# Attention products as sixteen 32x32 float32 tiles, first scores one batch ahead, row sums on ScalarE

## The reference

```python
row_zero = exp_v.sum(-1) == 0
q_exp = jnp.where(row_zero[..., None], 0.0, q[:, None, :])
self_feat = jnp.concatenate([exp_v, q_exp], -1) @ W_self.T + b_self
for d in range(2):                                   # adjacency and its transpose
    A = (adj_f if d == 0 else swapaxes(adj_f, 1, 2))[:, :, :20, :]
    cond, vb = A.sum(-1), A @ w_bias + b_bias
    kv = self_feat[:, :20]
    qh, kh = heads(self_feat @ Wq.T + bq), heads(kv @ Wk.T + bk)     # 16 heads of 32
    aff = einsum('bnhd,bmhd->bnhm', qh, kh) / sqrt(32)
    w = softmax(where(cond > 0, aff, NEG) + vb)      # over the 20 keys
    output += heads_out(einsum('bnhm,bmf->bnhf', w, kv), Wout) + bout
result = v + relu(self_feat + output)
```

## Time and profile before

| | us |
|---|---|
| time, median of 3 runs | 617.11 (617.08 to 618.52) |
| span of the profiled execution | 616.5 |
| own time of the profiled execution | not recorded; the median lies 0.6 above this span |
| PE busy | 606.8 (98%) |
| DVE busy | 527.0 (85%) |
| POOL busy | 436.2 (71%) |
| ACT busy | 386.7 (63%) |

### The profile page before, as it was taken

The page is one execution under the profiler, slowest core; times in us unless marked ns, Lnnn a source line. Parts: engine busy times, 40 slices in busy tenths (PEclk is TensorE's granted clock), DMA queues, the critical chain, the costliest instruction groups (busy, mean ns, idle before and its releaser), DMA issues.

```text
span 616.5 us, 10667 instructions
## 1 busy us (share of the span) xinstructions
PE 606.8 (98%) x4047; PEld 532.3 (86%) x4047; DVE 527.0 (85%) x770; ACT 386.7 (63%) x737; POOL 436.2 (71%) x400
## 2 busy tenths in 40 slices
PE   9999999999999999999999999999999999999995
PEld 6977898989898988989898898989898989889892
DVE  4898899999797989989797988888897979787675
ACT  4658647877566776757586755668574758653432
POOL 0301388876978886797986688989569798858852
PEclk9999999999999999999999999999999999999999
DMA  8976545846758672657775385857357676726061
GB/s 312 424 284 183 146 109 172 212 183 128 269 113 270 120 263 52 160 194 175 225 165 192 71 237 154 241 143 207 119 121 262 129 251 127 256 53 169 1 147 69
DMA packets 54466, 109.54 MB, mean 178 GB/s; under 512 B 27855, under 2 KB 37583, under 8 KB 47695
## 3 DMA queue, kind: packets, MB, share of 16 engines
q1 hardware_dynamic: 52254, 93.13, 47.7%
q0 software_dynamic: 2160, 15.73, 14.0%
HBM read 88.05 MB, written 20.78 MB: 177 GB/s over the span
## 4 chain that ended last, share of the span: by engine, by line
PE 94%; DVE 3%; POOL 1%; issue 1%; ACT 0%
PE aff L572 36%; PE gen L500 10%; PE gen L502 9%; PE gen L501 9%; PE aff L540 8%; PE tp L584 4%; PE aff L500 3%; PE aff L502 3%; PE aff L501 3%; PE aff L629 2%; PE gen L584 1%; PE tp L500 1%; PE tp L502 1%; PE tp L501 1%; PE tp L402 1%; DVE wol L1074 1%
## 5 line engine op out<-in xcount | busy, mean ns | idle before, releaser
L572 PE MATMUL aff<-gh,sfl 128*128 128x320 f32 x504 | 114.9, 309 | 0.0
L572 PE MATMUL aff<-gh,sfh 128*128 128x320 f32 x504 | 114.8, 309 | 0.0
L572 PE MATMUL aff<-gl,sfh 128*128 128x320 f32 x504 | 114.8, 309 | 0.0
L1279 POOL TENSOR_TENSOR xl<-x,xh 128x512 fp32r<-128x512 f32 x62 | 84.9, 1424 | 33.5 <-ACT xh L707 33.5
L1286 POOL TENSOR_TENSOR z<-cb,bx 128x640 f32<-128x640 f32 x64 | 100.6, 1607 | 10.7 <-PE tp L502 10.2
L500 PE MATMUL gen<-xh,w1h 128*128 128x512 f32 x256 | 104.0, 406 | 0.0
L502 PE MATMUL gen<-xh,w1l 128*128 128x512 f32 x256 | 100.5, 393 | 0.0
L501 PE MATMUL gen<-xl,w1h 128*128 128x512 f32 x256 | 99.8, 390 | 0.0
L880 ACT ACTIVATE z<-z 128x640 f32<-128x640 f32 x64 | 47.4, 741 | 79.1 <-POOL z L1298 77.2
L1283 POOL TENSOR_TENSOR sfl<-sff,sfh 128x512 fp32r<-128x512 f32 x48 | 61.2, 1293 | 46.0 <-ACT sfh L725 45.8
L1298 POOL TENSOR_TENSOR z<-z,mx 128x640 f32<-128x640 f32 x63 | 81.6, 1295 | 16.3 <-DVE mx L996 16.3
(11 more groups left out here) (163 smaller groups left out, 1215.3 us busy)
## 6 DMA issues: line engine op xcount, KB each, us to landing
x<-in_x SPq DMA_DIRECT2D x16, 1024.0 KB, 8.6
xn<-in_xn SPq DMA_DIRECT2D x31, 512.0 KB, 5.4
sff<-in_x POOLq DMA_DIRECT2D x15, 1024.0 KB, 8.4
out_y<-sff SPq DMA_DIRECT2D x15, 1024.0 KB, 4.9
msk<-in_mask SPq DMA_DIRECT2D x17, 880.0 KB, 7.4
cb<-c_scratch SPq DMA_DIRECT2D x16, 320.0 KB, 6.9
nz<-nz_scratch SPq DMA_DIRECT2D x16, 256.0 KB, 4.0
wkT<-in_wkT SPq DMA_DIRECT2D x4, 512.0 KB, 8.2
```

What stands on the lines that cost most here:

```text
L572: mm = nc.tensor.matmul(aff[:, t % 2, half, 0:SH], s, g[:, b - starts[group(b)], f, half * SH:(half + 1) * SH], start=(f == 0 and i == 0), ...
L1279: nc.gpsimd.tensor_tensor(xl[:, c, :], x[:, c, :], xh[:, c, :].bitcast(F32), ALU.subtract).then_inc(s_xl, 1)
```

## The change

Features are permuted on the host so that the four heads that share a set of 32 rows land in the four 32-column quadrants of one output bank. The values and the transposed weights stay in plain float32, with no split. `attend_rest` becomes four float32 matmuls of 32 rows and 128 columns, `attend` sixteen of 32 rows and 32 columns, all of 512 moving columns. They write into the banks `gen` and `tp` and not into `aff`. `evict_wt` becomes one plain copy on ACT, and `wt_low` goes. The scores of tile 0 of the next batch stand ahead of the attention products, with their `shift` on DVE, `sub_max` on POOL and exponential on ACT at the end of the body as well. `row_sums` moves from DVE to ACT in the loop, `x_high` to the end of the body; `label_mask` and `edge_terms` move later. Loads of values are 16 per batch where there were 12.

```diff
-            def attend_rest(b, slot, pair):
...
-                for k, (t, w) in enumerate(((0, wth), (0, wtl), (1, wth))):
-                    for j in range(HG):
-                        mm = nc.tensor.matmul(pv_bank(j), vr[r, t].rearrange("p h e -> p (h e)"), w[r, 0, :], start=(k == 0 and b < B - 1), stop=ends)
-            def attend(b, j):
...
-                mm = parts(pv_bank(j), tuple(va[:, j, t].rearrange("p h e -> p (h e)") for t in range(2)), (wt_high(j + 1), wt_rest(j + 1)), False, ends)
+            def attend_rest(b, slot):
...
+                for h in range(H4):
+                    r = slice(h * DH, (h + 1) * DH)
+                    nc.tensor.matmul(pv_bank(b, h), vr[r].rearrange("p j e -> p (j e)"), wt[r, 0, :], start=(b < B - 1), stop=False)
+            def attend(b, chunks):
...
+                for h in range(H4):
+                    r = slice(h * DH, (h + 1) * DH)
+                    for j in chunks:
+                        mm = nc.tensor.matmul(pv_bank(b, h)[j * DH:(j + 1) * DH], va[r, j, :], wt[r, j + 1, :], start=False, stop=True)
@@ TensorE, body of a batch
+                scores(b, slot, group(b), range(0 if b == 0 else 1, T))
...
                 transposes(b, slot, 4)
-                attend_rest(b, slot, pair)
-                for j in range(HG):
-                    attend(b, j)
+                scores(n, 1 - slot, group(n), range(1))
+                attend_rest(b, slot)
+                attend(b, range(HG))
@@ ScalarE
+            def row_sums(n, half, count):
+                for t in range(2):
+                    last = nc.scalar.activation(xn[:, t, :], xn[:, t, :], ACT.Copy, accum_out=rsum[:, 2 * half + t:2 * half + t + 1])
-                evict_wt(b, slot, 0)
+                if ahead == 2:
+                    row_sums(b + 2, 1, b * 32 + 64)
+                evict_wt(b, 0)
...
+                if ahead == 2:
+                    act.wait_ge(s_sf, n * FC + FC)
+                    x_high(n + 1)
+                act.wait_ge(s_sub, n * T + 1)
+                nc.scalar.activation(z[other][:, 0, :], z[other][:, 0, :], ACT.Exp).then_inc(s_exp, 1)
                 for j in range(HG):
                     relu(b, slot, j)
@@ VectorE
                 total(b, slot, 3)
                 add_query(n, other, 1)
+                if ahead == 2:
+                    label_mask(b + 2)
...
-                wt_low(b, slot, 4)
-                add_sf(b, slot, 0)
-                add_sf(b, slot, 1)
-                if ahead >= 1:
-                    sf_low(n, other)
-                for j in range(2, HG):
+                sf_low(n, other)
+                shift(n, other, 0)
+                for j in range(HG):
                     add_sf(b, slot, j)
@@ GpSimd
                     for t in range(T):
                         bias(n, other, t)
+                    sub_max(n, other, 0)
                     add_x(b, slot)
```

More of the change, by code:

```diff
@@ L554, in last_scores, with scores @@
                     mm.then_inc(s_aff, 1)
-            def scores(b, slot, pair):
+            def scores(b, slot, pair, tiles):
                 pe.wait_ge(s_gl, pair * GU + GU)
[L558 to L562, removed]
+                for t in tiles:
+                    if b > 0 or t >= 2:
                         pe.wait_ge(s_z, b * T + (t - 1))
@@ L859, in batch @@
                 next_g, pair = next_group(b) is not None, next_group(b)
+                if b == 0:
+                    act.wait_ge(s_sub, 1)
+                    nc.scalar.activation(z[0][:, 0, :], z[0][:, 0, :], ACT.Exp).then_inc(s_exp, 1)
+                    edge_terms(1)
                 if next_g:
                     k_blocks(pair)
-                if ahead >= 1 and b > 0:
-                    act.wait_ge(s_sf, b * FC + FC)
-                    x_high(n)
                 if ahead == 2 and b > 0:
@@ L871, in batch @@
                         add_bosum(b, slot, j)
-                for t in range(T):
+                for t in range(1, T):
                     if next_g and t == T - 1:
@@ L911, in batch @@
                     evict_g(pair, GU - 1)
-                for c in range(2, WC):
-                    evict_wt(b, slot, c)
-                if ahead >= 1:
-                    sf_high(n, other, FC - 1)
+                evict_wt(b, 2)
+                sf_high(n, other, FC - 1)
+                evict_wt(b, 3)
+                evict_wt(b, 4)
                 if b == 0:
@@ L1234, in batch @@
                     return
+                shift(b, slot, 3)
                 total(b, slot, 2)
-                if ahead >= 1:
-                    dve.wait_ge(s_out[other], (i + slot) * 16 + 16)
-                    add_query(n, other, 0)
+                dve.wait_ge(s_out[other], (i + slot) * 16 + 16)
+                add_query(n, other, 0)
                 if next_g:
@@ L1262, in batch @@
                 add_query(n, other, FC - 1)
-                wt_low(b, slot, 2)
-                wt_low(b, slot, 3)
-                wt_low(b, slot, 4)
-                add_sf(b, slot, 0)
-                add_sf(b, slot, 1)
-                if ahead >= 1:
-                    sf_low(n, other)
-                for j in range(2, HG):
+                sf_low(n, other)
+                shift(n, other, 0)
+                for j in range(HG):
                     add_sf(b, slot, j)
```

271 lines of the change are left out of this document (111 added, 160 removed).

## The result

The changed kernel takes 643.26 us (median of four runs, 643.0 to 643.75) against 617.1 us before: 1.042 times as long, 95% interval 1.040 to 1.043. The profiled execution has a span of 641.5 us, where before it had 616.5.

A forecast was written before the change was run, and what follows sets the result against it. TensorE's own work was taken to bound the kernel, with POOL reaching the same meeting point. Terms 14.8 + 1.1 + 6.5 - 1.6 = +20.8 us on the profiled 616.5 gave 637.3, median 638; range 601 to 651.

The forecast's parts named there:

- The block of tiles: TensorE's attention products, attend_rest and the sixteen tiles: forecast to take 2.15 us, 1.6 less than the earlier 3.76.
- The lower of the readings: Attention products: tiles work side by side, attend_rest 0.86 and sixteen tiles 0.86, 2.15 us with changes of tile shape.
- the two in which tiles wait for each other: Attention products: 3.4 us if ordered within a set of 32 rows, 9.9 in strict program order; tiles-in-order rival, chance 0.08.
- The new hand-offs: Chain from softmax of next tile 0 through relu, add_x, store and DVE's queue: period 33.2 us, was 31.35 or 31.10.
- The link through the store: After add_x: transfer 8.4 us, store 4.9, then add_query(b + 2, 0) done at 24.35; TensorE waits 2.6.
- the sign that I had named: The store's landing releases DVE's add_query, seen with a TensorE gap of about 2.6 us ahead of the third self_feat.
- eight periods without keys: Periods between attend_rest without key products: 1.85 us longer each, 14.8 in all.
- ninth, into the last batch: The period without keys leading into the last batch: no label work, ends 1.1 us later than before.
- five key periods: Periods with key products: products wait for g_low behind add_query(0) and label_mask, 1.3 us each, 6.5 in all.
- last batch, and what lies ahead of the first period: Last batch keeps its attention gain of 1.6 us; its tail and the prologue count nothing.
- That the hand-offs stay hidden: Rival: chain 3.5 us shorter per period, below TensorE's own 29.7; 15 x 1.6 come off, about 592; chance 0.24.
- half of them: Rival: links between engines overlap by 1 to 2 us per period more than counted, 612 to 626; chance 0.17.

The follow-up runs named there:

- experiment 3: Changed kernel with the sixteen 32x32 attention products of each batch but the last left out: 644.47 us, 1.045 of the kernel before.
- experiment 7: Changed kernel with label_mask moved from behind add_query(1) to ahead of total(2): 643.81 us; with nine unused products added in TensorE's wait: 634.40 us.
- experiment 6: Changed kernel with row sums moved back from ScalarE to DVE from the second batch on: 631.53 us, 1.025 of the kernel before.
- experiment 8: Changed kernel with relu before exponential, two x_low before add_x, label_mask before total(2), second row sums behind first copies: 608.87 us; first period also mended: 607.06 us.
- experiment 5: Changed kernel with the old order at the end of a batch on four engines, new tiles kept: 637.57 us, 1.033 of the kernel before.

## Why the prediction came out

**What bounds the kernel, right.** Two things followed from the trace of before: TensorE at 100%, and POOL reaching the same meeting point. A faster TensorE gained nothing: with the tiles left out altogether the time is the same (experiment 3).

**The block of tiles, right.** 2.15 forecast, 2.16 measured. The lower of the readings holds, against the two in which tiles wait for each other: column tiles run side by side as row tiles do. The Trainium skill (TensorE: Matmul & The Clock Gate, part 3, "The mechanism") says that matmuls start and end in program order. With a product's two records next to each other in that order, as the prediction took them, this would have made the block 9.9 us; the trace disagrees, with sixteen records that start within 0.12 us and their partners 0.45 us behind them. The trace does not show in which order the two records of a product stand in the program, so it refutes the two together and not the rule by itself.

**The new hand-offs, right in mechanism and close in size.** Counted from the end of the transposes (181.46 - 3.53 = 177.93):

| step | forecast | measured |
|---|---|---|
| `add_x` issued | 10.4 | 10.2 |
| `add_query(0)` done | 24.35 | 23.0 |
| `total(3)` done | 25.5 | 25.7 |
| `label_mask` done | 28.0 | 28.2 |
| row sums done | 31.2 | 31.3 |
| `transposes(2)` start | 31.8 | 31.8 |
| period | 33.2 | 33.3 |

The link through the store was mis-sized: I took its two durations from before (8.4 and 4.9), and they were 8.1 and 3.9 in this period, for the same bytes; why they were quicker I have not tested. So in this period the store has landed when DVE comes to `add_query(0)`, which starts right behind `total(2)`, and TensorE waits 0.98 ahead of the third `self_feat`, not 2.6; the sign that I had named, the store as what releases `add_query`, is seen in six of the eight periods and not in this one, and TensorE's wait is 2.17 at the most. The time came back one link further on, in a wait that I had not named: 1.14 ahead of the first transposes, on POOL's last `normalise`. That it did not matter is because what follows in DVE's queue passes through `total(3)`, and that was sized rightly, over POOL's row. `normalise_rest` costs 0.65 to 0.94 with its new pattern, and I had left it at 0.44.

**The sum, right in total, with terms off on both sides.** Spans of the two profiled executions, 641.5 - 616.5 = +25.0, against my +20.8:

| term | forecast | measured |
|---|---|---|
| eight periods without keys | +14.8 | +16.4 |
| ninth, into the last batch | +1.1 | +1.3 |
| five key periods | +6.5 | +10.1 |
| last batch, and what lies ahead of the first period | -1.6 | -2.8 |

The last row is two things. Of the first `attend_rest`, 4.1 later than before, 3.5 are the scores that moved ahead of it, and 0.6 I had put at nothing; the last batch gains 3.4, where I had 1.6. The total came as near as it did because this gain covers part of what the key periods lost.

Key periods are the term that failed, in its mechanism too. I had the second group of `key_products` wait because `g_low` stands behind `add_query(0)` and, from the third pair on, behind `label_mask` on DVE. There is a wait ahead of that group, of 1.75, but DVE is idle at that point:

```profile
236.00 2.35 DVE L964 TENSOR_TENSOR gl<-aff,gh 128x480 fp32r<-128x480 f32 x4 [1.77 <-ACT gh L745]
```

`g_low` waits for `evict_g` on ScalarE (L745), and that stands behind the first row sums. `label_mask` moved to another place left the wait at 1.75 (experiment 7); the row sums moved to DVE brought it down to 0.65 to 1.13 (experiment 6). I had counted the row sums once, ahead of the copies, and had not asked what stands behind their first half. On top of it the clock fell behind that wait in two of the three middle key periods and in the first: windows at 0.96, 42.2 long, against 41.5 at 1.00. The first also has a wait of 1.51 on DVE's `shift`. Against before the five are longer by 3.6, 2.4, 2.4, 1.7 and 0.1, where I had 1.3 for each.

**The rivals.** That the hand-offs stay hidden, or half of them, is refuted for this kernel; experiment 8 shows what it takes to hide them, about 2.9 us less per period, which is near the 3.5 that I had set as the point where it decides. It also shows that the rival's own time of 592 was too low: TensorE's own work is 30.05 us a period and not 29.7, and the total stays at 607.

## What to carry to other kernels

- Putting one stage of the next batch ahead of this batch's last products moves every engine's queue, not only the one that it is meant for. Follow the row of hand-offs that leaves the moved place (here `sub_max`, exponential, `relu`, `add_x`) and ask what stands behind each on its engine: here 5.4 us of `x_low` stood behind `add_x`, and half of them put into the wait ahead of it gave back 1.2 of the 2 us that a period had lost.
- When an engine at 100% is made faster, ask first which other engine meets it and with what margin. The mending was four changes of order, each of a piece of the chain that ended last, and it turned 1.042 into 0.987. The chain of one period, followed back, lists such pieces in one view.
- Read a wait's place exactly, down to the instruction behind it; one place off, a move into "idle time" made the longest wait longer.

## What the runs showed of the hardware

- A wait of TensorE can cost more than its length. Behind 2.44 us of idle time the products of 512 columns stood 0.43 apart instead of 0.235 (experiment 7), which is the lower of TensorE's two clocks, 1.2 GHz, for about 3.5 us; it cost 1.5 us. Nine throwaway products in the wait removed it. But the clock does not fall behind each such wait: behind 2.44 it fell in seven of eight periods of experiment 7, behind 1.75 in two of three like key periods of the changed kernel, behind 1.79 in one of four of experiment 6, behind 2.18 in two of four of experiment 5, and behind one of 2.62 in experiment 3 it stayed. So the length of one wait alone does not settle it, and what else counts stays open.
- A float32 product on a 32x32 tile appears as two records 0.43 to 0.45 us apart, and sixteen such tiles, four of rows by four of columns, cost 1.1 us together, round after round (three rounds: 3.3 us). The tiles of a column write to the same partitions of different banks.
- A copy of 512 columns with a row sum on ScalarE is a record of 0.61 and a read of the accumulator of 0.19, and a pair takes 1.32 us (207.89 to 209.21), where DVE's sum over the same data took 1.21.
